# Gram products over two coefficients in the two column halves of the array, instead of four coefficients over its whole width

## The reference

```
q = idwt2(depthwise 3x3 of each band of dwt2(x))      # 96x96 -> four 50x50 bands -> 96x96
k = depthwise 3x3 of (Wk x);  v = depthwise 3x3 of (Wv x)
q, k -> (image, 8 heads, 16 channels, 96*96);  both divided by their norms over the 96*96 points
attn = softmax(q k^T * temperature)                   # 16x16 per image and head
out = proj (attn v)
```

## Time and profile before

| what | us |
|---|---|
| median of 3 runs | 1515.75 |
| lowest, highest run | 1512.08, 1520.14 |
| the profiled execution, first to last instruction (its span) | 1510.3 |
| busy in the span: PE, PEld | 1236.3, 970.2 |
| busy in the span: DVE, ACT, POOL | 1122.9, 804.2, 242.7 |
| all Gram products (L969), busy on PE, 800 of them | 103.9 |

### The profile page before, as it was taken

How to read it: one execution, slowest core, us unless ns; L and a number is a source line. 1 busy time by engine, 2 the same in 40 slices (tenths; PEclk the granted TensorE clock), 3 DMA queues, 4 the chain that set the end, 5 groups by cost and what they waited for, 6 DMA issues and landing times. The chain is left out here.

```text
span 1510.3 us, 35911 instructions
## 1 busy us (share of the span) xinstructions
PE 1236.3 (82%) x12644; PEld 970.2 (64%) x12644; DVE 1122.9 (74%) x1899; ACT 804.2 (53%) x1382; POOL 242.7 (16%) x241
## 2 busy tenths in 40 slices
PE   1999757889999898998989999863799999799910
PEld 0555447889888788988989988832355555455500
DVE  6777348899999999998999999905676663153384
ACT  0677654656566565665655666401224424766473
POOL 6100021122222222222222213112000000000000
PEclk9999967889899999998998989976799999899965
DMA  9966853434344343443434344035877531000069
GB/s 331 416 274 274 261 136 83 117 80 122 84 122 123 88 130 84 121 128 79 129 89 120 98 108 109 34 131 196 288 266 255 177 102 61 0 0 1 0 239 402
DMA packets 148701, 221.22 MB, mean 146 GB/s; under 512 B 115625, under 2 KB 116789, under 8 KB 144193
## 3 DMA queue, kind: packets, MB, share of 16 engines
q1 hardware_dynamic: 137456, 152.26, 32.9%
q0 software_dynamic: 6480, 47.19, 8.3%
q10 hardware_dynamic: 4608, 19.67, 3.8%
HBM read 131.84 MB, written 87.20 MB: 145 GB/s over the span
## 5 line engine op out<-in xcount | busy, mean ns | idle before, releaser
L879 DVE SCALAR_TENSOR_TENSOR b_value_sum<-b_vin,b_vtaps,b_value_sum 128x576 f32<-128x576 f32 x384 | 309.6, 806 | 0.1
L1602 PE MATMUL b_conv_bank<-b_sign,wsign 128*128 (+1 forms) x1728 | 296.7, 329 | 10.3 <-ACT b_sign L1382 7.7
L835 ACT CAST b_feat<-b_bank 96x400 f16<-96x400 f32 x255 | 124.9, 490 | 266.9 <-PE b_bank L923 266.9
L1602 PEld LDWEIGHTS b_conv_bank<-b_sign,wsign 128*128 128x128 bf16 x1728 | 168.6, 98 | 141.6 <-issue 29.7
L921 PE MATMUL b_bank<-b_tkh,b_kt 96*96 96x100 f16 x1536 | 234.3, 216 | 13.6 <-DVE b_feat L886 11.2
L922 PE MATMUL b_bank<-b_tkl,b_kt 96*96 96x100 f16 x1536 | 233.0, 215 | 0.0
L923 PE MATMUL b_bank<-b_tkh,b_kt 96*96 96x100 f16 x1536 | 232.9, 215 | 0.0
L921 PE MATMUL b_bank<-b_yh,b_tmh 96*96 96x200 f16 x768 | 209.3, 273 | 25.6 <-DVE b_yl L886 12.0
L921 PEld LDWEIGHTS b_bank<-b_tkh,b_kt 96*96 96x96 f16 x1536 | 201.6, 131 | 18.8 <-DVE b_feat L886 15.5
L923 PE MATMUL b_bank<-b_yh,b_tml 96*96 96x200 f16 x768 | 206.8, 269 | 0.0
L922 PE MATMUL b_bank<-b_yl,b_tmh 96*96 96x200 f16 x768 | 206.4, 269 | 0.0
(11 more groups left out here) (211 smaller groups left out, 2440.9 us busy)
## 6 DMA issues: line engine op xcount, KB each, us to landing
b_vin<-value_projection_scratch SPq DMA_DIRECT2D x32, 686.0 KB, 5.5
value_projection_scratch<-b_vout ACTq DMA_DIRECT2D x24, 784.0 KB, 4.6
keys_scratch<-b_khl SPq DMA_DIRECT2D x24, 784.0 KB, 3.5
b_kt<-keys_scratch SPq DMA_DIRECT2D x128, 147.0 KB, 2.8
b_xraw<-in_x SPq DMA_DIRECT2D x128, 144.0 KB, 4.8
values_scratch<-b_vacc SPq DMA_DIRECT2D x32, 576.0 KB, 3.2
b_values<-values_scratch SPq DMA_DIRECT2D x48, 384.0 KB, 3.9
out<-xs SPq DMA_DIRECT2D x25, 576.0 KB, 6.8
```

What stands on the lines that cost most here:

```text
L835: nc.scalar.copy(*target(n, 0, k)).then_inc(s_hi, 1)
L879: nc.vector.scalar_tensor_tensor(whole if t == 8 else part, src, vtaps[:, t:t + 1], whole if t == 1 else part, ALU.mult, ALU.add).then_inc ...
L1602: ins = nc.tensor.matmul(cbank[k % NBK][:, 0:CH].rearrange("p (r c) -> p r c", c=W), p["wsign"][nth // NIMG][:, t * C:(t + 1) * C], padded ...
```

## The change

`RUN` goes from 4 to 2, so that a block holds two coefficients: each matmul has 64 stationary and 128 moving columns, and a head has 200 of them in place of 100. Blocks with even number write PSUM partitions 0 to 63, those with odd number partitions 64 to 127 (`GTILES` = 2), which are the two column halves of the array. A product's output is a quarter of the size per half, so the four images of a head fit into one bank; there is one part in place of two, and one copy to `b2_gout` per head. The pieces hold 20 products each and stand behind n9, n14, n19 of A, n4, n9, n14, n19 of B and n4, n9, n14 of C. The one copy stands behind ACT's copy of n15 in step C. The stores of a head are two of 64 rows in place of four of 32 rows. In `block_attention` the shapes are the same as before.

```diff
-MT, MPB, RUN = 7, 3, 4
+MT, MPB, RUN = 7, 3, 2
+GTILES = 2
+GROWS = 2 * HD * RUN * GTILES
...
-        GPARTS = NIMG // 2 + 1
+        GPARTS = 2
...
                 for r in range(RUN):
-                    rows = slice(r * 2 * HD, (r + 1) * 2 * HD)
+                    rows = slice(r * 2 * HD * GTILES, (r + 1) * 2 * HD * GTILES)
...
-        units = [[(2 * e + im, blk) for im in range(2) for blk in range(S2B // RUN)] for e in range(GPARTS - 1)]
-        PER = 10
-        START, COPY_AT, NULL_AT = [0, 6], [5, 11, 14], 12
+        units = [(im, blk) for im in range(NIMG) for blk in range(S2B // RUN)]
+        PER = 20
+        COPY_AT, NULL_AT = [10, 14], 12
...
-                    ins = nc.scalar.copy(gout[:, 2 * e:2 * e + 2, :, :].rearrange("p b r f -> p b f r"),
-                                         gbank[:].rearrange("p (b f r) -> p b f r", b=2, r=RUN))
+                    ins = nc.scalar.copy(gout[:].rearrange("p b r f -> p b f r"),
+                                         gbank[:].rearrange("p (b f r) -> p b f r", b=NIMG, r=RUN))
...
-            def gram_part(head, parity, e, first, last):
+            def gram_part(head, parity, first, last):
                 if first == 0:
-                    pe.wait_ge(s_gout, head * GPARTS + (e + 1))
-                for n, (im, blk) in list(enumerate(units[e]))[first:last]:
-                    half = im % 2 * (4 * HD * RUN)
+                    pe.wait_ge(s_gout, head * GPARTS + 1)
+                for n, (im, blk) in list(enumerate(units))[first:last]:
+                    tile = blk % GTILES
                     f = feat[:, parity, im, blk, :, :].rearrange("w f r -> w (f r)")
-                    ins = nc.tensor.matmul(gbank[:, half:half + 4 * HD * RUN], f[:, 0:2 * HD * RUN], f,
-                                           start=(blk == 0), stop=(blk == S2B // RUN - 1))
-                    if n == len(units[e]) - 1:
+                    ins = nc.tensor.matmul(gbank[tile * GTILE:(tile + 1) * GTILE, im * 2 * GTILE:(im + 1) * 2 * GTILE],
+                                           f[:, 0:GTILE], f, start=(blk < GTILES), stop=(blk >= S2B // RUN - GTILES))
+                    if n == len(units) - 1:
                         ins.then_inc(s_gram, 1)
...
-            for e in range(GPARTS - 1):
-                gram_part(HEADS - 1, (HEADS - 1) % 2, e, 0, len(units[e]))
+            gram_part(HEADS - 1, (HEADS - 1) % 2, 0, len(units))
             gram_null(HEADS - 1)
```

More of the change, by code:

```diff
@@ L119, in constants @@
     first_of_group[np.arange(NG) * GC, np.arange(NG)] = 1
-    pick = np.tile(np.concatenate([np.eye(2 * HD), 2 * np.eye(2 * HD)], 1), (RUN, 1)).astype(np.float32)
+    pick = np.tile(np.concatenate([np.eye(2 * HD), 2 * np.eye(2 * HD)], 1), (RUN * GTILES, 1)).astype(np.float32)
     return {
@@ L479, in block_grams @@
         NM = GC * 6
+        GTILE = 2 * HD * RUN
         xraw = sb("b2_xraw", [H, 2, CI * W])
@@ L495, in block_grams @@
         vtaps = sb("b2_vtaps", [C, 9])
-        gout = sb("b2_gout", [2 * HD * RUN, NIMG, RUN, 4 * HD])
+        gout = sb("b2_gout", [GROWS, NIMG, RUN, 4 * HD])
         gcor = sb("b2_gcor", [HD, NIMG * HD])
@@ L1023, in body @@
                             need(at["u", GC - 1])
-                        for e, first in enumerate(START):
-                            if first <= piece and (piece - first) * PER < len(units[e]):
-                                gram_part(gram, parity, e, (piece - first) * PER, (piece - first + 1) * PER)
+                        if piece * PER < len(units):
+                            gram_part(gram, parity, piece * PER, (piece + 1) * PER)
                         if piece == NULL_AT:
@@ L1065, in block_attention @@
         HI = HEADS * NIMG
-        pick = sb("b3_pick", [2 * HD * RUN, 4 * HD])
+        pick = sb("b3_pick", [GROWS, 4 * HD])
         eye = sb("b3_eye", [HD, HD])
         ones = sb("b3_ones", [HD, HD])
-        gram = sb("b3_gram", [2 * HD * RUN, HI, 4, HD])
+        gram = sb("b3_gram", [GROWS, HI, 4, HD])
         gcor = sb("b3_gcor", [HD, HI, HD])
@@ L1666, in build @@
                 block_stats_and_projections(nc, d, p)
-            d["gram"] = scratch("gram_scratch", (2 * HD * RUN, HEADS * NIMG * 4 * HD))
+            d["gram"] = scratch("gram_scratch", (GROWS, HEADS * NIMG * 4 * HD))
             d["gcor"] = scratch("gram_null_scratch", (HD, HEADS * NIMG * HD))
```

## The result

The changed kernel takes 1592.18 us (median of 4 runs, 1583.64 to 1593.61). Beside it the kernel before took 1513.91 (4 runs); the ratio of the runs is put at 1.0502, with a 95% interval of 1.0467 to 1.0537. That is slower, as forecast, but by 78 us where 20 were forecast, and outside the range. The profiled execution spans 1590.8 us, 80.5 more than before, and its granted clock over the whole span is 0.838, where it was 0.899. A run more than 1.5% above the fastest of its kernel counts as slow and is left out of the medians and ratios that follow, which concerns one run each of two experiments.

What follows compares the result with a forecast made beforehand. DVE was taken to bound the steps, with little room on PE. +4.0 a head (+28.0 in all) less 7.9 at the block's end gave +20.1 us: 1530.4 profiled, 1536 us forecast; 8-in-10 range 1499 to 1558.

Steps and rivals of the forecast that it cites:

- The forecast's 0.75 for a piece: PE's piece of 20 products: 10 pairs at 0.057 plus 0.18 for two changes of shape, 0.34 us less than before.
- the halves queue: Rival, chance 0.22: the column halves don't run side by side, a piece takes 1.32 us, about 1518 us in all.
- The leads: How far POOL's subtraction starts before DVE's ninth tap: 0.83 us in step B, 0.88 in step C.
- The turning point: Latest POOL start that still blocks DVE's ninth tap, put at the start of DVE's subtraction of n10.
- POOL stays late: Rival, chance 0.20: products run side by side, but POOL's subtraction blocks no ninth tap in B and C; 1500 us.
- +2.1 a step for the block: Steps B and C: DVE's ninth tap waits for POOL's subtraction, 2.9 us in place of 0.81, in each of 7 heads.
- -0.6 from C to D: DVE's 0.63 us of idle time goes, as the copy before D's first tap is gone; per head.
- -0.5 from D to A: DVE waits there for PE at half clock; one or two pieces shorter by 0.34 us save 0.5 a head.
- The clock ... I give each of the two new blocks an even chance: +0.9 a head: After the blocked taps in B and C: PE's clock falls with even chance, each fall costing 0.9 us.
- every new block brings the clock down for long: Rival, chance 0.09: B and C become 27.0 us like D to A, +56.5 us in all, 1572 us.
- the forecast's own range: 1522 to 1548 us: no clock fall gives 1530, one at every block 1542, and 6 either side for the blocks' size.
- The end of the block: The last head's uncovered products take 9.0 us in place of 15.6 (-6.6), and two stores fewer save 1.3: -7.9.

## Why the prediction was wrong

**Right: the products and the pieces.** The lines are the job before a piece in step C, first of the kernel before (its piece is in the earlier trace rows), then of the changed one, with the piece and the job behind it:

```profile
564.05 0.38 PE L931 MATMUL b_bank<-b_rk,b_key_place 126*96 126x168 f16 x3
...
595.38 0.38 PE L934 MATMUL b_bank<-b_rk,b_key_place 126*96 126x168 f16 x3
595.69 0.75 PE L972 MATMUL b_gram<-b_feat 96*64 96x128 f16 x20
596.37 0.24 PE L924 MATMUL b_bank<-b_tkh,b_kt 96*96 96x100 f16 x1
```

From job to job it was 1.31 us and is 0.99: 0.32 less, where 0.34 was forecast. The forecast's 0.75 for a piece holds both changes of shape; the first lies ahead of the piece (0.31 to its start, where it was 0.22), so 0.75 stands beside 0.68 + 0.09 = 0.77. In one half a piece takes 1.23 to the next job, so the rival "the halves queue" is out. The Trainium skill's page "TensorEngine Tiling (Array Packing)", section Restrictions and Gotchas, which spoke for it (no fast weight load with column tiling), may hold, but no loss by it shows here: the pieces cost what the sum gave.

**Right: POOL becomes early and blocks, in B and C.** The leads were forecast as 0.83 and 0.88 and are 0.76 and 0.77; the tap was 2.9 and is 2.98 and 2.96. Both causes (two pieces ahead in C; pieces and the copy in B) are shown by the runs with 7 of 10 products. The turning point was put 0.13 to 0.18 us too early, which decided nothing here. The rival "POOL stays late" is out. The Trainium skill's page "SBUF — State Buffer", section Who interferes with whom, says that a DVE instruction with two inputs in SBUF and a GpSimd instruction reading SBUF exclude each other, and that the order of issue decides who waits. The trace agrees on the first: the ninth tap reads `b_vin` and `b_vacc`, both in SBUF, and is the one that loses 2 us; taps that read `b_value_sum`, in PSUM, keep 0.8. On the order it agrees from a lead of 0.36 us on; with 0.05 to 0.31 POOL starts first and still waits, so by the profile's starts the order alone does not decide.

**Right in size: +2.1 a step for the block, -0.6 from C to D.** The run with the wait filled shows them without falls: the window from C to D is 23.95, where 22.53 + 2.1 - 0.6 makes 24.0. The -0.5 from D to A was not tested by itself.

**Wrong: "The clock ... I give each of the two new blocks an even chance: +0.9 a head".** The loss of the steps is 91.0 us. The other terms, +2.1 + 2.1 - 0.6 - 0.5 for seven heads, make 22; what is left for the clock is 69, about 9.9 a head in place of 0.9. The step that failed is this term, in how often the clock falls and in what a fall costs. I gave a fall an even chance in two of a head's four steps; it comes in 26 of the 27 windows. And I took its price from A (0.9), though D showed a dear one as well. Here it is D's that repeats: B to C and C to D took 27.13 and 26.60 in place of my 24 (21.78 + 2.1, and 24.0), some 3 us each, and the mean of the 27 steps, 733.0 / 27 = 27.1, shows that A is no longer spared (A to B takes 25.8 to 27.5 in six of the seven heads). The argument against the rival "every new block brings the clock down for long" was false: the piece behind n14 that was to cover PE's wait is there (573.82 to 574.50), but the wait comes a job later, at n16, and takes 1.54 us in spite of it. It is longer than D's 1.29. That rival, which I gave 0.09, is the case that came, and its 1572 is still 20 too low: it left A to B at 24, and a step of 23.65 is now the exception. (A slip beside it: the forecast's own range, 1530 less 6, starts at 1524 and not at 1522; nothing hangs on it.)

**The end of the block.** The 200 products take 8.17 us where 9.0 was forecast, in place of 15.6 with the wait between the parts; the stores 1.26 in place of 2.54, the 1.3 saved as forecast. The products start 22.8 us after the last step does, where it was 21.4. So 7.4 + 1.3 - 1.4 = 7.3 of the 91.0 come back there, where 7.9 were forecast. The rest down to the span's 80.5 lies behind the block: from the end of its last store to the end of the span it is 507.0 us before and 503.6 after. What makes these 3.4 was not looked into.

**What stays open.** Filling PE's wait shows that most falls need the wait; it does not show which waits bring the clock down, and for how long. In the changed kernel a wait of the same kind passed without a fall (the window from 550.71), with the extra work ahead of n18 eleven did, and in three of the kernel before's steps A waits of 1.08 to 1.29 us did. With 7 of 10 products and the copy moved the blocks are as many and as long, and yet the time is 1555.6 and not 1592. I did not take these apart.

## What to carry to other kernels

Making an engine faster moves the starts of all that it releases. Before crediting the saved time, follow the release to the next pair of instructions that exclude each other, and ask who will now come first; a transfer or copy that was harmlessly late may be harmful when early. If a wait is then fixed by order, an explicit wait on the engine with spare time can cost nothing: here POOL's subtraction starts 1.00 us behind the start of the tap, and the wait alone takes 3.1% off the kernel before, where the change on top of it takes 0.9%. And where a wait of PE has been seen once with a long stretch at half clock behind it, the same wait elsewhere may cost that stretch too: a forecast should price both cases and not the cheapest one in the trace alone.

## What the runs showed of the hardware

- Two products of 64 columns side by side, with 128 moving columns each, take 0.68 us for ten pairs, to the start of the next job; twenty in one half take 1.23.
- Of two instructions that exclude each other the first to start does not always win: POOL, released 0.05 to 0.31 us before the tap, waits for the whole tap (3.84 to 4.08 us in place of 3.1); released 0.36 before it, it wins.
- 32 useless products in PE's wait of some 1.5 us make the kernel 82 us faster (1592.2 to 1510.1), behind the wait 13 us (1578.7), and the clock of the steps goes from 0.80 to 0.98 and 0.88: PE's standing still is dear through the clock, although DVE was the engine that was late. Not every such wait brings the clock down.
